# Four small edits at the seams of a Toeplitz convolution and fp8 feed-forward kernel: a load moved, a rounding moved, warm-up matmuls and the last row tile's matmuls reordered

## The reference

```python
K = 2.0 * jnp.einsum('hn,hnl->hl', Ct, jnp.exp(P)).real            # (32, 512)
y = jnp.fft.irfft(uf * kf[None], n=n)[..., :Lq] + u * D[:, None]
y = y * mask[:, None, :]
...
gate_out = _fake_quant_fp8_linear(y, gate_w, gate_in_scale, gate_w_scale)
up_out = _fake_quant_fp8_linear(y, up_w, up_in_scale, up_w_scale)
hidden = jax.nn.silu(gate_out) * up_out
return x + _fake_quant_fp8_linear(hidden, down_w, down_in_scale, down_w_scale)
```

## Time and profile before

| what | value |
|---|---|
| median of 3 runs | 323.59 us (323.27 to 323.6) |
| the profiled execution's own time | 324.86 us |
| its span, first to last instruction | 323.2 us |
| PE busy | 310.3 us, 96% |
| DVE busy | 303.1 us, 94% |
| ACT busy | 206.5 us, 64% |

### The profile page before, as it was taken

One profiled execution on the slowest core, in us unless ns is written; L12 is line 12 of the kernel. 1 busy time (PEld: TensorE's weight loads), 2 busy tenths in 40 slices (PEclk: granted clock), 3 DMA queues, 4 the chain that ended last, 5 costly groups with the idle time before them and its releaser, 6 DMA issues.

```text
span 323.2 us, 4716 instructions
## 1 busy us (share of the span) xinstructions
PE 310.3 (96%) x1591; PEld 161.8 (50%) x1591; DVE 303.1 (94%) x460; ACT 206.5 (64%) x318; POOL 13.7 (4%) x25
## 2 busy tenths in 40 slices
PE   1979999999999999999999999999999999999996
PEld 1456655545455454555455454555545554444443
DVE  6969999999999999999989999899998999999894
ACT  4938788278765868376863958366864859545550
POOL 3031000000001000010001000010000000010010
PEclk9999999999999999999999999999999999999999
DMA  6869999500001690067401690046600770070028
GB/s 201 170 174 218 240 292 363 220 1 2 0 0 13 128 357 26 1 117 243 159 0 16 126 360 19 0 80 202 239 0 0 132 261 0 3 130 0 0 26 235
DMA packets 14015, 38.42 MB, mean 119 GB/s; under 512 B 1470, under 2 KB 6558, under 8 KB 11052
## 3 DMA queue, kind: packets, MB, share of 16 engines
q1 hardware_dynamic: 8412, 26.61, 23.9%
q0 software_dynamic: 5584, 11.57, 20.5%
HBM read 33.93 MB, written 15.81 MB: 154 GB/s over the span
## 4 chain that ended last, share of the span: by engine, by line
PE 77%; DVE 15%; issue 3%; DMA 3%; ACT 2%; DVEq 0%; SPq 0%
PE gate_ps L604 20%; PE up_ps L604 20%; PE down_ps L542 17%; PE y_ps L528 15%; DVE hv L917 3%; DVE yq L901 2%; DVE ht L925 2%; DVE yt L890 2%; DVE hq L934 2%; PE down_ps L558 2%; PE y_ps L558 1%; DMA toep<-kpad_scratch 1%; DVE ym L882 1%; PE y_ps L655 1%; DMA kpad_scratch<-hq 1%
## 5 line engine op out<-in xcount | busy, mean ns | idle before, releaser
L415 ACT ACTIVATE sil<-gate_ps,fac 128x512 f32<-128x512 f32 (+1 forms) x88 | 59.8, 681 | 71.4 <-PE gate_ps L604 70.5
L604 PE MATMUL gate_ps<-yq,wg 128*128 128x512 bf16 (+2 forms) x372 | 89.5, 363 | 0.5 <-DVE hv L917 0.3
L604 PE MATMUL up_ps<-yq,wu 128*128 128x512 bf16 (+2 forms) x372 | 89.5, 363 | 0.0
L528 PE MATMUL y_ps<-xt,toep 128*128 128x512 f32 (+1 forms) x248 | 78.1, 434 | 0.0
L917 DVE SCALAR_TENSOR_TENSOR hv<-up_ps,fac,sil 128x512 f32<-128x512 f32 (+1 forms) x88 | 65.5, 744 | 6.9 <-ACT sil L415 3.5
L542 PE MATMUL down_ps<-wd,hq 128*128 128x512 bf16 (+1 forms) x264 | 67.9, 379 | 0.0
L397 ACT ACTIVATE hc<-hv 128x1024 f32<-128x1024 f32 (+1 forms) x48 | 47.0, 980 | 17.1 <-DVE hq L934 16.7
L604 PEld LDWEIGHTS gate_ps<-yq,wg 128*128 128x128 bf16 x372 | 36.0, 100 | 41.0 <-issue 2.2
L528 PEld LDWEIGHTS y_ps<-xt,toep 128*128 128x128 f32 x248 | 45.8, 190 | 20.0 <-issue 2.4
L604 PEld LDWEIGHTS up_ps<-yq,wu 128*128 128x128 bf16 x372 | 36.3, 100 | 38.3
L925 DVE SCALAR_TENSOR_TENSOR ht<-hc,hv 128x1024 f32<-128x1024 f32 (+1 forms) x48 | 54.2, 1129 | 0.9 <-ACT hc L397 0.9
(11 more groups left out here) (163 smaller groups left out, 133.8 us busy)
## 6 DMA issues: line engine op xcount, KB each, us to landing
xt<-in_xT SPq DMA_DIRECT2D x8, 1024.0 KB, 7.8
out<-in_x SPq DMA_DIRECT2D x7, 1024.0 KB, 5.7
out<-res POOLq DMA_DIRECT2D x7, 1024.0 KB, 7.7
toep<-kpad_scratch SPq DMA_DIRECT2D x6, 1024.0 KB, 10.1
toep<-kpad_scratch SPq DMA_DIRECT2D x8, 256.0 KB, 5.1
wd<-in_down POOLq DMA_DIRECT2D x1, 1280.0 KB, 21.9
xt<-in_x SPq DMA_DIRECT2D x1, 1024.0 KB, 7.4
out<-xt SPq DMA_DIRECT2D x3, 256.0 KB, 3.2
```

Of the source, the lines that this page charges most:

```text
L415: nc.scalar.activation(sil[b][0:w, :], gate_ps[b][0:w, :], ACT.Silu, scale=fac[0:w, S_GATE:S_GATE + 1]).then_inc(silu_done, 1)
L528: last = nc.tensor.matmul(y_ps[h % 2][:, d * P:L], toep[par][:, h, d * P:(d + 1) * P], xt[par][:, h, 0:L - d * P], start=(d == 0), stop=(d ...
L604: mm = nc.tensor.matmul(ps[b][0:w, cols], wt[:, k, c * P:c * P + w], yq[par][:, version, k, cols], start=(k == 0), stop=(k == LB - 1))
```

## The change

Four edits. `WARM`: ten warm-up matmuls instead of eight ahead of the second k group, one instead of two behind it. The load of x for block 1 is issued behind block 0's toep rows. In block 1, pair 4 of block 0 is rounded in slot 1 and not 0, and its clip and all that pair 5 needs behind the sum are done in slot 2 (so it was already in the last block). In the last down matmuls, the first six chunks of row tile 3 come ahead of the last chunks of tiles 0 and 1.

```diff
-WARM = (1, 1, 8, 2)
+WARM = (1, 1, 10, 1)
...
             load_x_t(0, 0)
-            load_x_t(1, 1)
...
             for h in range(HB):
                 sp.dma_start(toep[0][:, h], toep_d[0, :, h]).then_inc(toep_first[h], 16)
+            load_x_t(1, 1)
             store_k(1)
...
-                                    (2, range(6), full), (0, range(8, CH), full), (1, range(8, CH), full),
-                                    (2, range(6, CH), full), (3, range(CH), slice(0, 3 * P)),
+                                    (2, range(6), full), (3, range(6), slice(0, 3 * P)),
+                                    (0, range(8, CH), full), (1, range(8, CH), full),
+                                    (2, range(6, CH), full), (3, range(6, CH), slice(0, 3 * P)),
                                     (3, range(CH), slice(3 * P, L))):
...
             def slots(g, par, ahead, before, plan):
                 first = before is None
-                behind = g == NBLK - 1
+                behind = g - 1 in SUM_BEHIND
```

## The result

The changed kernel takes 325.54 us (median of 6 runs, 325.39 to 325.92), the kernel before 323.37 (6 runs, 323.15 to 323.60). The ratio is 1.0068, with an interval of 1.0055 to 1.0081: 2.17 us slower. Forecast were 324.3 and a range of 322.8 to 325.2. The side was right, the time lies outside the range. Two of the twelve runs of experiment 6 (328.63 and 329.60 us) and one of the twelve of experiment 11 (327.92) were in a slower state, with a granted clock of 0.990 to 0.995, and the ratios leave them out.

What follows compares the result with a forecast made beforehand. DVE was taken to set the pace through block 0 into block 1, then PE to the last block. The terms -0.20+1.26-0.35=+0.71 on the median 323.59 gave 324.30 us, with a range of 322.8 to 325.2.

Steps and rivals of the forecast that it cites:

- the moved load: Start, SP's queue: first convolution 0.20 us earlier, block 1's first toep row landing at 28.6, in time; sum -0.20.
- Rival 3: Block 1's first toep row takes 7.9 us, lands at 31.8, 1.5 after PE asks: 325.7 us, chance 0.10.
- The gain of the load: Chain of k store, toep row, first convolution: between 0 and 0.3 us earlier, taken as 0.20.
- fixed cost of about 2.0 us: Skill's rule per DMA, given for GpSimd's path: the first store's gain would be 0 and the sum 0.20 higher.
- The left-overs: Block 1, DVE: idle 1.04 and 0.28 us waiting for ACT, then moved work of 1.26 delays PE's chunk 7: +1.26.
- The down matmuls' wait for the clip: Block 1, PE: chunks 8 and 9 wait about 1 us for clip 4, at no extra cost while chunk 7 waits for DVE.
- Rival 1: Block 1: moved DVE work costs nothing or helps if product 2 can start before about 73.3; 322.6 or 323.0 us, chance 0.18.
- The first rule at the top of the prediction: Idle time put into DVE before the hand-over to PE reaches the end in full, since PE has no slack.
- The tail: Last block: PE's hole of 0.47 us before clip 5 goes; taken as -0.35, between 0.20 and 0.47.
- Its low case: Last output piece queues behind the three of 256 KB ahead and gains some 0.25 us.
- The warm-up: Start, PE: two more matmuls, 0.44 us, covered by 2.00 us of idle time before the first convolution; cost 0.
- fall of the clock: Rival: one warm-up matmul less before PE's pause drops the clock to 1.2 GHz, some 2.4 us more: 326.7, chance 0.03.

Runs made afterwards that it cites:

- experiment 6: Block 1's x load issued behind the second k store, all else as in the kernel before: 323.39 us for 323.51, ratio 0.9993.
- experiment 11: Block 1's x load split, 512 KB ahead of the second k store and 512 KB behind it, against the kernel before: 323.28 us, ratio 1.0004.
- experiment 2: Only block 1's x load moved behind block 0's toep rows, against the kernel before: 324.56 us, ratio 1.0044.
- Experiment 4: Only the warm-up matmuls changed (10 and 1), against the kernel before: 323.45 us, ratio 1.0001.
- Experiment 7: Against the kernel before, only the second rounding moved behind block 1's product 1; clip 4, rounding 5 and clip 5 stay ahead of product 2: 323.45 us for 323.51.
- experiments 1: Only the new order of block 0's left-overs in block 1, against the kernel before: 324.78 us for 323.41, ratio 1.0039.

## Why the prediction was wrong in size

**The step that failed** is the moved load: "The nearest row is that of the first; with some 1 us for the weights that now run beside it, I take 28.6. So 0, with a late row as a rival." It costs 1.15 us by itself where the sum had -0.20. Three things in it were off.

- The rows came later. In the changed kernel the first of block 1 landed at 29.8 and in experiment 2 at 30.0. The issue near 23.9 was about right (23.39), but from there the row took 6.4 and 6.7 us, not 3.7 plus 1. The earlier trace rows held a row with 7.9 for toep loads beside the weights. It was the nearer one: from 22 to 72 us the DMA engines are 87% busy, while the row that took 3.7 had set out near 21.3, at the end of the stretch in which they were 9% busy. Even in experiment 6 the first row took 6.65 us (19.85 to 26.50); it was in time because it set out 3.5 us earlier.
- The deadline was earlier. "The first is needed at 30.30" was read from an execution whose first row had come late by chance (19.09; in the other traces with the load where it was 17.3 to 17.7). Everything behind it was shifted too. In the changed kernel PE asks at 28.52 and in experiment 2 at 28.44, so there was 1.8 us less to spare than the forecast counted. A landing at 28.6, as forecast, would have been near enough in time; and by the late deadline the 29.8 that came would have been in time as well.
- What had been late was counted as standing. That execution was 1.3 us above the median of the runs shown, and the text took its stretches to be the median's. The question to ask was where that difference lay: it is the wait of 2.00 us ahead of 19.14, which in the other traces is 0 to 0.6.

Rival 3 named this mechanism, at 0.10 and 1.4 us. Its price was right (1.42 us from the first convolution to chunk 7 in experiment 2), its condition ("from 6.4 us on") reckoned with the wrong deadline. From the true one, 28.5, a row that sets out at 23.4 is late from 5.1 us on, and the two traces with the whole load ahead of the store show 6.4 and 6.7. That its 325.7 lies so near the 325.54 measured is partly luck: it counted 1.4 for the row but 0.20 for a gain of some 0.4 and 0.35 for a tail that gave half of it or less.

The gain of the load, "between 0 and 0.3 us earlier", is 0.42 in the traces of experiments 2 and 4; the medians can't part it from the loss. Over all traces the first convolution starts at 16.99 to 17.27 in the four with the load moved and at 17.42 to 17.76 in the nine others besides the forecast's. The k store of 8 KB lands in 1.4 us in those four, for 2.0 in the forecast's trace and 1.7 to 1.9 in the others. It had no x load in flight before it in either case: with the load where it was, that load had landed by 11.4 and the store is issued at 12.2 to 12.3. What differs is the traffic: from 12.2 to 13.6 us the DMA engines are 62 to 81% busy there, and 4% with the load moved, where the first weights have all landed by 12.4. So the fixed cost of about 2.0 us, which the prediction weighed from the Trainium skill ("DMA: Bandwidth & Descriptors", the anatomy of one DMA) and which is given there for GpSimd's path, doesn't hold for this store on SP's queue: the measurement decides, at 1.4.

A rule of the same page bears on the loss. The Trainium skill ("DMA: Bandwidth & Descriptors", "Queues, rings and completion order") says that SP's DMAs share one row of rings, and that each DMA engine takes a ring's descriptors in their order. By that, 16 KB behind 1 MB must wait for it; the traces agree, with 6.3 us behind the load and 2.5 ahead of it.

**The left-overs** were right in mechanism and size. Forecast: idle 1.04 and 0.28 ahead of product 2 and the sum, released by ACT, and +1.26. The traces have 1.05 and 0.20, and 1.05 and 0.19, the time +1.37. The down matmuls' wait for the clip, forecast as about 1 us that costs nothing, is 1.21 us, and it does cost nothing, since PE still waits 0.37 for DVE at chunk 7. Experiment 7 undoes the cause and loses the cost. Rival 1 fell at the condition that it named itself: sil of chunk 2 doesn't come earlier, since ACT's run to it starts at DVE's first rounding (4.29 us from that rounding to sil before, 4.28 now). The first rule at the top of the prediction, that idle time put into DVE before the hand-over arrives in full, holds too: 1.24 us of it moved chunk 7 by 1.25.

**The tail** was right in what it does on PE (the hole gone, the add 0.47 us earlier) and too high in what it gives: -0.35 forecast, -0.16 measured with an interval that takes in 0. Its low case, "if it queues behind the others it gains some 0.25", reckoned with the last block's own pieces alone. Block 6's accumulation, which holds these up, is not in its working; without it the same edit gives 0.33.

**The warm-up** was right at 0, but its cover was not what the text named: the idle time of 2.00 us is usually 0 to 0.6. Nor does PE have 0.44 us more to do ahead of the first convolution: both groups of warm-up matmuls stand ahead of it, so two more and one less make 0.22. Experiment 4's first convolution came at 17.52, within the 17.4 to 17.8 of the other executions with the old load. Its second k store was issued at 17.83, for 17.07 to 17.66, and its block 1 row at 26.57 was still 2.1 us early. No fall of the clock was seen: it was 1.00 in the stretches read.

With the measured values the forecast's sum would read +1.15+1.37-0.16+0.04 on 323.4, that is 325.8, for 325.54. The two losses don't quite add: from the first convolution to chunk 7 the changed kernel takes 68.84 us, 2.33 more than the 66.5 of before, where experiments 1 and 2 take 1.25 and 1.42 more, 2.67 together. Why 0.3 of it is saved was not tested.

## What to carry to other kernels

Before a deadline is read from a profile, compare the profiled execution's own time with the median; if they differ, find the place of the difference first and read deadlines without it. Two executions are compared best from an instruction behind that place, as here from the first convolution. A big load put ahead of a small store on the same queue costs whatever waits for the store, and the landing time to reckon with is that of transfers in the traffic of that stretch, not of the first one at the start. Work moved behind a product helps only if the product can really start earlier: look at what else it waits for, and at what will wait for the moved work.

## What was not expected of the hardware

- A single load lands late by chance, and that moves the whole execution. The kernel before had 19.09 us for its first toep row once and 17.3 to 17.7 in nine other traces with the load in the same place. Its load for block 4 took 10.2 us once and 11.9 once, and then PE stood 1.2 us for it. Each made its execution some 1.5 us longer: both profiled executions, at 324.86 and 324.95, lie 1.4 to 1.5 us above the median, and above the 322.96 to 324.38 of the kernel's timed runs beside the experiments. Why a load is late was not found.
- A store's time depends strongly on what is in flight and what is ahead of it. 8 KB took 1.4 us to land with the DMA engines 4% busy and 1.7 to 2.0 with them 62 to 81% busy. 16 KB took 6.3 us behind a load of 1 MB on the same queue, 5.3 behind half of it, and 2.5 ahead of it.
- One accumulation of 1 MB on GpSimd's queue, in flight when the last output sets out, lengthens the landing of pieces of 256 KB on SP's queue from 2.1 to 3.3 us. Of the 0.47 us that PE gained in the new tail, 0.09 reached the last landing with it, and 0.44 without it.
